# Splitting the next block's tokens behind the last inner chunk in a graph-attention and mixture-of-experts kernel

## The reference, cut to what matters

```python
h2 = _ln(x, ln2_g, ln2_b).reshape(-1, d)
gate_logits = h2 @ Wg
w, sel = jax.lax.top_k(gate_logits, K)               # K = 1, eight experts
...
hid = jax.nn.relu(jnp.einsum('nd,edf->enf', h2, W1) + b1[:, None, :])   # 768 -> 3072
y = jnp.einsum('enf,efd->end', hid, W2) + b2[:, None, :]                # 3072 -> 768
moe = jnp.einsum('ne,end->nd', combine, y)
return x + moe.reshape(b, t, d)
```

## Time and profile before

| | |
|---|---|
| median of 3 runs | 1289.19 us (1286.11 to 1289.38) |
| the profiled execution | 1285.7 us, its span 1284.0 us |
| expert loop | from about 766 us to the end of the span |
| TensorE busy / VectorE / ScalarE / GpSimd | 1074.4 / 804.6 / 557.2 / 340.0 us |

### The profile page before, as it was taken

How to read it: one execution, slowest core, us unless ns; L and a number is a source line. 1 busy time by engine, 2 the same in 40 slices (tenths; PEclk the granted TensorE clock), 3 DMA queues, 4 the chain that set the end, 5 groups by cost and what they waited for, 6 DMA issues and landing times.

```text
span 1284.0 us, 19500 instructions
## 1 busy us (share of the span) xinstructions
PE 1074.4 (84%) x6126; PEld 685.3 (53%) x6127; DVE 804.6 (63%) x1503; ACT 557.2 (43%) x740; POOL 340.0 (26%) x175
## 2 busy tenths in 40 slices
PE   0459877899969958999999605989998989898997
PEld 0335546754755745558887502545555545454554
DVE  1366767876462874428876517896224998889732
ACT  0336755630331114417762207774113676677611
POOL 3000000037000340207000145563001655656400
PEclk9979998999979978997999657999999999899999
DMA  8720020002330440011000099997002999999600
GB/s 319 293 89 0 0 76 24 1 1 99 96 50 1 113 84 13 1 44 48 2 2 1 8 222 339 343 343 269 21 25 64 352 321 354 327 351 341 226 25 27
DMA packets 98242, 170.50 MB, mean 133 GB/s; under 512 B 38395, under 2 KB 38667, under 8 KB 98194
## 3 DMA queue, kind: packets, MB, share of 16 engines
q1 hardware_dynamic: 88002, 145.20, 33.3%
q0 software_dynamic: 6016, 16.80, 4.1%
q10 hardware_dynamic: 4176, 7.87, 1.9%
HBM read 153.05 MB, written 18.79 MB: 134 GB/s over the span
## 4 chain that ended last, share of the span: by engine, by line
PE 63%; DVE 13%; issue 9%; DMA 5%; SPq 3%; ACT 3%; POOL 3%; DVEq 2%; POOLq 0%; ACTq 0%
PE psum L1316 30%; PE psum L1526 13%; PE psum L1505 12%; PE psum L1305 3%; DMA area<-in_L_gnn_a_dst_dram 2%; PE psum L1354 2%; POOL area L628 1%; DMA sorted_tokens<-area,smalls 1%; PE psum L1514 1%; SPq L441 1%; SPq L439 1%; DMA low<-in_L_ffn_W_dram 1%; DVE low L1275 1%; DVE smalls L911 1%; DVE low L1017 1%
## 5 line engine op out<-in xcount | busy, mean ns | idle before, releaser
L1316 PE MATMUL psum<-area,low 128*125 128x256 f16 (+2 forms) x1080 | 248.5, 392 | 21.2 <-DVE low L1096 10.9
L1526 PE MATMUL psum<-area,low 128*128 128x384 f16 x1296 | 232.3, 339 | 27.0 <-DVE low L1282 16.7
L628 POOL TENSOR_TENSOR area<-low,area 128x1536 f16<-128x1536 f32 x48 | 189.2, 3944 | 179.0 <-ACT area L841 178.7
L1505 PE MATMUL psum<-area,low 128*128 128x512 f16 x972 | 220.7, 383 | 9.5 <-DVE area L1248 9.5
L1316 PEld LDWEIGHTS psum<-area,low 128*125 128x125 f16 (+1 forms) x1080 | 150.5, 150 | 114.2 <-issue 63.1
L841 ACT ACTIVATE area<-low 128x1536 f16<-128x1536 f32 x144 | 203.3, 1470 | 8.5 <-DMA low<-in_L_ffn_W_dram 6.9
L1248 DVE TENSOR_TENSOR area<-low,area 128x1536 f16<-128x1536 f32 x96 | 198.2, 2107 | 10.8 <-ACT area L841 10.8
L1526 PEld LDWEIGHTS psum<-area,low 128*128 128x128 f16 x1296 | 130.3, 101 | 117.1 <-issue 44.8
L1316 PE MATMUL psum<-area 125*125 125x64 f16 (+9 forms) x1076 | 163.7, 305 | 12.1 <-DVE area L1234 8.0
L1505 PEld LDWEIGHTS psum<-area,low 128*128 128x128 f16 x972 | 95.9, 99 | 121.2 <-issue 14.7
L1316 PEld LDWEIGHTS psum<-area 125*125 125x125 f16 (+2 forms) x1076 | 118.9, 161 | 41.7 <-issue 14.1
(11 more groups left out here) (198 smaller groups left out, 1206.7 us busy)
## 6 DMA issues: line engine op xcount, KB each, us to landing
low<-in_L_ffn_W_dram SPq DMA_DIRECT2D x144, 768.0 KB, 6.6
area<-in_L_gnn_W_dram SPq DMA_DIRECT2D x2, 3072.0 KB, 26.5
area<-in_L_gnn_Wr_dram SPq DMA_DIRECT2D x2, 3072.0 KB, 31.0
sorted_tokens<-area POOLq DMA_DIRECT2D x3, 1792.0 KB, 20.4
sorted_totals<-area POOLq DMA_DIRECT2D x3, 1792.0 KB, 41.9
low<-sorted_tokens ACTq DMA_DIRECT2D x11, 384.0 KB, 5.7
low<-in_x_dram SPq DMA_DIRECT2D x10, 375.0 KB
low<-sorted_totals ACTq DMA_DIRECT2D x9, 384.0 KB, 2.9
```

The costliest lines, as they stand in the source:

```text
L628: pool.tensor_tensor(low_, raw_view(u), high_, ALU.subtract).then_inc(pool_low_ok, 1)
L1316: ins = pe.matmul(place(name)[0:parts, at:at + w], left(q), right(q)[:, at:at + w], start=(q == 0), stop=(q == k - 1))
L1505: ins = pe.matmul(psum[:, (c % 2) * BANK:(c % 2 + 1) * BANK], ht[x_][:, k, :], w1_s[c][w_][:, k, :], start=(k == 0 and x_ + w_ == 0), stop ...
L1526: ins = pe.matmul(psum[:, (4 + q) * BANK:(4 + q) * BANK + D // 2], hidT[c % 2][x_][:, j, :], w2_s[c][w_][:, j, q * D // 2:(q + 1) * D // 2 ...
```

## The change

In step 6, ScalarE makes the high part of the next block's tokens behind the high part of inner chunk 5 instead of in front of it, and VectorE makes their low part behind the low part of chunk 5 instead of between the relu and the low part. No instruction is added or removed.

```diff
@@ scalar, block_steps
-                if s_ == C:
-                    tokens_high(b + 1)
                 if 1 <= s_ <= C:
                     c = s_ - 1
                     act.wait_ge(relu_ok, b * C + (c + 1))
                     act.wait_ge(hid_used, b * C + (C + c - 1))
                     act.activation(hidT[c % 2][0], v3(relu, CK), ACT.Copy).then_inc(hidhi_ok, 1)
+                if s_ == C:
+                    tokens_high(b + 1)
@@ vector, block_steps
                     ins.then_inc(relu_ok, 1)
-                    if c == C - 1:
-                        tokens_low(b + 1)
                     dve.wait_ge(hidhi_ok, b * C + (c + 2))
                     dve.tensor_tensor(hidT[c % 2][1], v3(relu, CK), hidT[c % 2][0],
                                       ALU.subtract).then_inc(hid_relu, 1)
+                    if c == C - 1:
+                        tokens_low(b + 1)
```

## The result

The changed kernel takes 1295.26 us (median of 6 runs, 1289.38 to 1298.7) against 1288.32 us before (6 runs, 1284.84 to 1289.81). The ratio is 1.0056, 95% interval 1.0029 to 1.0083: slower by half a per cent. The spans of the two profiled executions are 1293.9 and 1284.0 us.

A forecast was written before the change was run, and what follows sets the result against it. Where weights are converted, VectorE and TensorE are nearly full, and VectorE's queue gates the next pass. Terms: 5 x (0.87 - 0.87) + 4 x 0 = 0, plus clock: 1289.2 + 1.3 = 1290.5 us, range 1284.5 to 1297.

The forecast's parts named there:

- What bounds: Before a new expert, VectorE's queue sets the next pass's first second product, a constant 20.15 us after the last one's start.
- VectorE's 0.87 us: Before a new expert, chunk 5's low part ends earlier, so the last second product starts 0.87 us earlier, five times.
- ScalarE, the loads, the four other passes: ScalarE's high parts 0.78 us late, two loads behind moved instructions, and passes whose successor has the same expert: each cost 0.
- Rival C: ScalarE's 0.78 us delay reaches VectorE's queue before a new expert: up to 3.9 us slower, 1293.1 us; chance 0.06.
- The 0.87 us given back: TensorE meets VectorE's gate at the next pass's first second product at the same time as before: sum 0.
- Rival B: The 0.87 us is passed on to the next pass's first second product: 4.35 us faster, 1284.8 us; chance 0.12.
- The clock: Longer idle before the next pass's first second product brings one more fall to half clock, 1.7 to 2 us.
- rival A: Freed time becomes low clock in most of the five passes, 2 to 2.9 us each: 1296 us; chance 0.22.
- no change: Whole-kernel time within the edges of 0.02 faster and 0.02 slower; chance 0.62.
- The three idle times forecast at 2.8 to 3.2 us: TensorE's idle before the next pass's first second product grows to 3.16, 2.82 and 2.84 us in three of five passes.
- the other two, put at 1.56 us: TensorE's idle before the next pass's first second product stays at 1.56 us in two of five passes.
- The lower bound of a fall: Least cost of one clock fall, read from slowed last second products: 5.67 - 4.06 = 1.6 us.

The follow-up runs named there:

- e4: Kernel before, with 12 useless filling matmuls on TensorE ahead of the first second product of an expert's first pass; 1287.6 us, ratio 0.9984.
- e7: Kernel before, with the third unit of slice 0 subtracted by VectorE instead of GpSimd; 1295.85 us, one run, read for its trace only.
- e8: Changed kernel, with the third unit of slice 0 subtracted by VectorE instead of GpSimd; 1298.68 us, one run, read for its trace only.
- e1: Kernel before with only VectorE's half of the change, ScalarE in its old order; 1297.56 us, ratio 1.0061.
- e2: Kernel before with only ScalarE's half of the change, VectorE in its old order; 1294.01 us, ratio 1.0029.
- e3: Changed kernel, with 20 useless filling matmuls on TensorE ahead of the first second product of an expert's first pass; 1288.31 us, ratio 0.9984.
- e9: Changed kernel, with 8 useless filling matmuls on TensorE ahead of the first second product of an expert's first pass; 1289.45 us, ratio 0.9999.
- e10: Changed kernel, with 20 filling matmuls ahead of the last second product of a pass before a new expert; 1298.5 us, ratio 1.0061.

## Why the prediction was right or wrong

**What bounds: right.** The prediction had read a constant interval between the two second products. It held in every run that left VectorE's load alone: 20.15 us with the old order on VectorE, 21.02 with the new one, within 0.02. The one exception is a pass of e4, 20.59 us, where the last second product was slow (6.92 us) and the filling made TensorE late.

**VectorE's 0.87 us: right to the hundredth.** The idle went from 3.33 to 2.46, and e7 and e8 show that it is GpSimd's hold. The Trainium skill, "SBUF — State Buffer", section "Who interferes with whom", says that issue order decides which of the two blocks. The trace agrees: the instruction that VectorE issued behind GpSimd's start was the long one in either order, L1260 with 2.82 us before and L1280 with 1.69 after, and L1280 ended 0.55 us behind GpSimd's end, as worked out.

**ScalarE, the loads, the four other passes: right.** Cost 0 in the trace. Rival C is out for this change, since e1 has the loss without ScalarE's move; e8 shows that its mechanism is real once GpSimd's hold is away.

**The 0.87 us given back: right.** Rival B is out by the interval of 21.02 us in all five passes.

**The clock: right mechanism, wrong size.** The step that failed is the term for the clock: "I take one more fall (the 2.29 becomes 3.16) at 1.7 to 2". There were three more, five of five, and they were dearer: 2.03 us each on the mean (10.16 / 5) against 1.68. I had 1.3 us for the median and the runs show 6.9. So rival A, given 0.22 and 1296 us, is what happened, and "no change" was the wrong favourite. The measured 1295.26 us lies in the stated range only because the range was drawn to take in rival A.

The three idle times forecast at 2.8 to 3.2 us were each counted as a fall, and each was one. What went wrong is the other two, put at 1.56 us. They were 2.78 and 2.77, and both fell, for 1.39 + 1.68 = 3.07 us together. I had kept the long last second products of 6.93 and 6.94 us in front of them. How long these are varies: behind the idle of 3.33 us in before, e2 and e4 they take 4.06 to 6.94 us, and behind that of 2.46 us in after, e1, e3 and e9 never more than 5.74. In the changed kernel they took 5.72 and 5.74 us in these two passes, and what TensorE saves at the first place it idles at the second. I said that such a saving brings no gain, and missed that it brings a loss. The rest is size: the one fall that I did add cost 2.88 us, and the two old ones grew by 0.85 together, for which the sum had nothing.

Two slips lie beside this. The lower bound of a fall, 1.6 us, left out the first pass, whose 5.33 us product gives 1.3; two of the falls measured, 1.39 and 1.41 us, lie under 1.6. And by the chances given to the rivals, faster and slower come to 0.08 and 0.30 where 0.10 and 0.28 are stated.

That the growth of the idle time is the cause, and not something that goes with it, is shown by e3 and e9; that the place decides, by e10.

## What to carry to other kernels

When a wait of TensorE is shortened, look for the next wait and ask who sets its end. If that is another engine, the time saved only moves idle from one place to the next, and there it may cost the clock, as here. Measure the interval between the two starts over several passes: if it is constant while the work inside varies, the gain will not get through. And when an instruction is long now and then, look whose hold it waits for before counting on its removal: the hold goes over to its successor.

Filling matmuls in an idle time that comes every time cost nothing that could be measured and kept the clock: the changed kernel got back from 1.0056 to 0.9984 of the time before, 0.9968 to 0.9999. Where the idle time is sometimes too short for them they make TensorE late, by 0.44 us in one pass of e4. Against the kernel before this is no gain worth having.

## What the runs showed of the hardware that was not expected

How often the clock falls goes with the idle time, but not by it alone. Take the second place in the ten traces of before, after, e1 to e4 and e7 to e10, and as idle time what a row has in front of the second product, behind the filling where there is one. No fall followed any of the 12 idle times under 1.5 us; 3 of 13 between 1.8 and 2.4 us were followed by one (1.95, 1.97 and 2.39, but not 2.29, nor a second 1.95 in e4); and 18 of 25 over 2.7 us. In after, e1 and e10 it was 15 of 15, in e7 none of four, at 2.91 to 3.25 us. A fall added 1.3 to 2.9 us to a product of 4.06 us. What sets e7 apart stays open. The clock falls at the first place too: behind 2.45 to 2.48 us of idle in after, e1, e3 and e9, 14 of 20 last second products were slow.
